# One PSUM bank in place of two for the spread B rows of a Mamba scan, with the small means and variances beside it one state earlier

## What is computed

```python
x = x + conv(_ln_c(x), ...)      # a Mamba block over 4 sequences
t = t + ffn(_ln_t(t), ...)       # top-2 of 8 experts, and a shared expert
def step(h, inputs):             # 256 inner channels, 16 states
    dt_t, B_t, C_t, u_t = inputs
    dA = jnp.exp(dt_t[:, :, None] * A)
    h = dA * h + (dt_t * u_t)[:, :, None] * B_t[:, None, :]
    y = jnp.einsum('bdn,bn->bd', h, C_t)
    return (h, y)
```

## Time and profile before

| | before |
|---|---|
| median of 3 runs | 2801.65 us |
| lowest and highest | 2800.4 and 2802.36 us |
| the profiled execution, its time | 2802.32 us |
| its span, first to last instruction | 2800.7 us |
| around the span | 1.6 us |
| TensorE busy | 2437.4 us, 87% |
| VectorE busy | 1409.5 us, 50% |
| GpSimd busy | 1127.7 us, 40% |
| ScalarE busy | 1012.9 us, 36% |
| mean granted clock of TensorE | 0.962 of 2.4 GHz |

### The profile page before, as it was taken

One profiled execution on the slowest core, in us unless ns is written; L12 is line 12 of the kernel. 1 busy time (PEld: TensorE's weight loads), 2 busy tenths in 40 slices (PEclk: granted clock), 3 DMA queues, 4 the chain that ended last, 5 costly groups with the idle time before them and its releaser, 6 DMA issues.

```text
span 2800.7 us, 28349 instructions
## 1 busy us (share of the span) xinstructions
PE 2437.4 (87%) x7648; PEld 1257.2 (45%) x7649; DVE 1409.5 (50%) x1767; ACT 1012.9 (36%) x1971; POOL 1127.7 (40%) x959
## 2 busy tenths in 40 slices
PE   5788888878888888877999999999999999999962
PEld 3345445444444444444444444444444444444431
DVE  1899999998999999996321111111111111111125
ACT  3776766776667767762100100010011001100000
POOL 2788787787787887874003400000000000000015
PEclk7999999999999999999999999999999999999985
DMA  9212112212122222222024311230202202030026
GB/s 297 71 66 68 64 62 68 66 66 70 60 66 69 66 63 71 66 68 72 28 103 131 117 34 39 97 112 22 112 22 112 112 23 112 26 116 23 22 71 211
DMA packets 92975, 220.27 MB, mean 79 GB/s; under 512 B 11217, under 2 KB 34361, under 8 KB 89537
## 3 DMA queue, kind: packets, MB, share of 16 engines
q1 hardware_dynamic: 77840, 138.79, 15.2%
q0 software_dynamic: 15024, 80.23, 8.1%
HBM read 172.25 MB, written 46.73 MB: 78 GB/s over the span
## 4 chain that ended last, share of the span: by engine, by line
PE 56%; DVE 25%; issue 10%; ACT 5%; POOL 2%; DVEq 1%; DMA 0%; ACTq 0%; SPq 0%; POOLq 0%
PE pair L1442 31%; DVE WALL L1005 15%; PE single L1454 15%; DVE pair L988 8%; PE pair L1323 4%; PE single L1229 2%; PE pair L1224 2%; ACT z L818 1%; POOL WALL L614 1%; PE pair L1424 1%; ACT WALL L770 1%; DVEq L270 1%; PE single L1291 1%; PE pair L1316 0%; DVE X L948 0%
## 5 line engine op out<-in xcount | busy, mean ns | idle before, releaser
L1442 PE MATMUL pair<-WALL,z 128*128 (+1 forms) x1952 | 855.0, 596 | 31.0 <-ACT z L818 29.6
L527 POOL TENSOR_TENSOR WALL<-WALL 128x768 f32<-128x768 f32 x384 | 696.5, 1816 | 243.5 <-DVE WALL L1005 229.2
L1005 DVE TENSOR_TENSOR_SCAN WALL<-WALL,carry,pair 128x384 f32<-128x384 f32 x640 | 613.4, 1000 | 20.5 <-ACT WALL L770 4.2
L1323 PE MATMUL pair<-WALL,ident 128*128 128x384 f32 x1536 | 581.1, 504 | 3.1 <-DVE pair L988 3.1
L1442 PEld LDWEIGHTS pair<-WALL,z 128*128 128x128 f32 x1952 | 366.4, 190 | 483.4 <-issue 480.1
L1127 DVE TENSOR_TENSOR dtu<-dt,pair 128x512 f32<-128x512 f32 x122 | 83.9, 688 | 803.2 <-ACT dt L824 797.1
L770 ACT ACTIVATE WALL<-dt,An 128x384 f32<-128x384 f32 x768 | 424.1, 605 | 75.0 <-DVE WALL L1005 56.5
L988 DVE TENSOR_TENSOR pair<-dtu,pair 128x768 f32<-128x768 f32 x384 | 368.8, 960 | 51.8 <-POOL dtu L456 15.8
L824 ACT ACTIVATE dt<-pair 128x512 f32<-128x512 f32 x122 | 72.8, 597 | 828.4 <-PE pair L1442 828.4
L1323 PEld LDWEIGHTS pair<-WALL,ident 128*128 128x128 f32 x1536 | 293.9, 198 | 138.2 <-issue 22.1
L594 POOL DMA_DIRECT2D WALL<-in_L_ffn_w_dram x21 | 13.9, 666 | 826.3 <-PE single L1454 824.7
(11 more groups left out here) (213 smaller groups left out, 2037.9 us busy)
## 6 DMA issues: line engine op xcount, KB each, us to landing
WALL<-crows SPq DMA_DIRECT2D x192, 384.0 KB, 3.4
WALL<-in_L_ffn_w_dram POOLq DMA_DIRECT2D x24, 2048.0 KB, 13.5
u<-xrows SPq DMA_DIRECT2D x61, 256.0 KB
xrows<-zrow SPq DMA_DIRECT2D x43, 256.0 KB, 2.7
yrows<-expx SPq DMA_DIRECT2D x31, 256.0 KB
yrows<-onex SPq DMA_DIRECT2D x30, 256.0 KB
WALL<-in_L_ffn_sw_dram POOLq DMA_DIRECT2D x3, 2048.0 KB, 13.0
X<-in_x_dram SPq DMA_DIRECT2D x4, 1152.0 KB, 7.8
```

Source lines behind the costliest of these rows:

```text
L527: pool.tensor_tensor(hC[m], hs[:, (NS * j + n) % HRING, :, :], Cs[G % 3][:, n % CG, :].unsqueeze(1).to_broadcast([P, HALF, T]), ALU.mult). ...
L1005: scan = nv.tensor_tensor_scan(hs[:, m, h, :], dA[(NS * j + n) % AHEAD][:, h, :], Dt[:, h, 0:T], init, ALU.mult, ALU.add)
L1323: last = mm(Yt[:, h, 0:T], ident[:, :], hC[n % RING][:, h, :], start=(n == 0), stop=(n == NS - 1))
L1442: last = mm(bank[2 * w + q][:, :], xT[k][:, r, :], WALL[:, ds(off + (w * RR * I + r * I + q * 512), 512)], start=(r == 0), stop=(r == RR - 1))
```

## The change

`Bb` becomes one bank. TensorE, once the product of state n is done, spreads the row of state n + 1 in place of n + 2. VectorE takes the variances in states 1 and 3 (before: 2 and 4), and the two `centre` steps in states 9 and 13 (before: 10 and 14). TensorE still makes the means in states 0, 2, 8 and 12, and all its other work stays in its state.

```diff
--- before.py
+++ after.py
@@ -143,7 +143,7 @@
         single = [ctx.enter_context(nc.psum_tensor(f"single{k}", [P, 512], fp32)) for k in range(2)]
         bank = [pair[k // 2][:, k % 2, :] for k in range(6)] + [single[k][:, :] for k in range(2)]
         Yt, Dt = pair[0], pair[2]
-        Bb = [bank[2], bank[3]]
+        Bb = bank[2]
         M0, M1 = bank[6], bank[7]
         STAT = T
 
@@ -971,22 +971,22 @@
                     for n in range(NS):
                         i = NS * g + n
                         m = (NS * j + n) % HRING
-                        stat = Bb[n % 2][:, STAT:STAT + CP]
+                        stat = Bb[:, STAT:STAT + CP]
                         v.wait_ge(m_B, i + 1)
-                        if front1 and n == 2:
+                        if front1 and n == 1:
                             front_variance(g + 2, stat)
-                        if late and n == 4:
+                        if late and n == 3:
                             back_variance(g - 2, stat)
-                        if front0 and n == 10:
+                        if front0 and n == 9:
                             centre(g + 3, b if j < JC - 3 else b + 1, (j + 3) % JC, f_mean, f_cen, cen, stat, f_seq, g + 3)
-                        if behind and n == 14:
+                        if behind and n == 13:
                             centre(g - 1, bb, bj, b_mean, b_cen, cen2, stat, b_lps, g - 1)
 
                         if n == 0:
                             v.wait_ge(f_dtu, g + 1)
                         after(v, m_h, i)
                         nv.tensor_tensor(Dt[:, :, 0:T], dtu[k][:, :, :],
-                                         Bb[n % 2][:, 0:T].unsqueeze(1).to_broadcast([P, HALF, T]),
+                                         Bb[:, 0:T].unsqueeze(1).to_broadcast([P, HALF, T]),
                                          ALU.mult).then_inc(m_dBu, 1)
 
                         if behind and n == 3:
@@ -1313,7 +1313,7 @@
             pe.wait_ge(s_x, 16 * (B - 1))
 
             def spread(g, j, n):
-                mm(Bb[n % 2][:, 0:T], sel[:, n, :], S[j % 2][:, :], start=True, stop=True).then_inc(m_B, 1)
+                mm(Bb[:, 0:T], sel[:, n, :], S[j % 2][:, :], start=True, stop=True).then_inc(m_B, 1)
 
             def add_y(g, n):
                 pe.wait_ge(m_hC, NS * g + n + 1)
@@ -1328,8 +1328,7 @@
                     last = mm(Yt[:, h, 0:T], Dg[:, h, :], u[k][:, h, :], start=False, stop=False)
                 last.then_inc(m_du, 1)
             pe.wait_ge(f_lo, 1)
-            for n in range(2):
-                spread(0, 0, n)
+            spread(0, 0, 0)
 
             def batch(b, first, last):
                 for j in range(JC):
@@ -1359,12 +1358,11 @@
                             pe.wait_ge(b_x, g)
                             pe.wait_ge(f_cen, g + 4 if front0 else NCH)
                             mean_of(xchunk(bb, bj), b_mean, stat)
-                        if n < NS - 2:
-                            spread(g, j, n + 2)
+                        if n < NS - 1:
+                            spread(g, j, n + 1)
                         elif front:
-                            if n == NS - 2:
-                                pe.wait_ge(f_lo, g + 2)
-                            spread(g + 1, j + 1, n + 2 - NS)
+                            pe.wait_ge(f_lo, g + 2)
+                            spread(g + 1, j + 1, 0)
 
                         if n < 3:
                             if behind:
```

## The result

| | before | changed |
|---|---|---|
| median of 4 runs | 2801.34 us | 2857.19 us |
| lowest and highest | 2800.4 and 2802.36 us | 2852.41 and 2859.09 us |
| the profiled execution, its time and span | 2802.32, 2800.7 us | 2855.74, 2854.1 us |

The ratio is 1.0197, with a 95% interval of 1.0179 to 1.0214. The change makes the kernel 2% slower. The forecast was 2855 us and slower.

What follows compares the result with a forecast made beforehand. VectorE, 95% busy in the scan stage, was taken to set the pace. A 57.75 us wait at the back `centre`, less 4.6 us returned, made 53.2 us on 2802.3: 2855 us, range 2836 to 2872 us.

Steps and rivals of the forecast that it cites:

- Part 1: Scan stage, one bank: the later spread stays hidden behind VectorE's two scans, with 0.5 us to spare; cost nothing.
- rival C: Scan stage: the spread comes late, in all 384 states (near 3055 us) or in part (2873 us); chance 0.06.
- Part 2: Variances in states 1 and 3, front `centre` in state 9: the wait for the spread row covers their means; cost nothing.
- Part 3: Back `centre` in state 13 waits for `gate_logits` in 22 chunks, 1.5 us or, at TensorE's low clock, 3.15; 57.75 us.
- Part 4: From state 13 TensorE has no arrears, so VectorE's old waits at `gate_y` and `centre` vanish; 4.6 us come back.
- The sum: Whole kernel: 57.75 us lost less 4.6 us returned, 53.2 us, giving 2855 us, 1.9% slower.
- B: State 12: only 0 to 8 chunks run at TensorE's low clock; 2830 to 2843 us; chance 0.10.
- A: State 12: nearly every chunk, 18 to 22, runs at TensorE's low clock; 2866 to 2871 us; chance 0.14.
- D: Scan stage: the old waits at `gate_y` and `centre` vanish and nothing replaces them; faster, 2797 us; chance 0.02.
- E: State 13: the back `centre` finds its count reached, so nothing moves; 2802 us; chance 0.02.
- The 22 waits at L924: VectorE's `centre` waits for `gate_logits` behind the scans of state 12, 1.5 or 3 us each, 45 to 65 us total.
- L988 was to wait under 1 us for spreads: Scan stage: VectorE's waits at source line L988 for TensorE's spread row stay under 1 us in total.

## Why the prediction was right

- **Part 1, the bank, at nothing.** Right by itself: one bank alone is at 1.0003. The 0.5 us of cover in a state with a mean held at full clock: from 430 to 690 us of that run, most of it at full clock, VectorE waited 0.2 us in all for a spread. The price given for half clock, 0.75 us, should be 2.87 - 2.15 = 0.72, which makes rival C's 18 us 17.3. The rule on rotating banks in the Trainium skill (Perfetto Trace Analysis, Matmuls) would have had each state pay. The run with one bank alone decides against it here: two scans, 1.92 us, lie between two readings of the bank.
- **Part 2, the variances and the front `centre`, at nothing.** Right within 0.1%: 2805.46 against 2804.35 us.
- **Part 3, the wait of the back `centre`.** The mechanism, its count of 22 and both prices were right: 1.50 us forecast and 1.41 to 1.55 measured, 3.15 forecast and 2.96 to 3.23 measured. The count of slow chunks was wrong: I raised the trace's 13 to 15 for the new idle time behind `gate_logits`, and the profiled execution had 6, the next one 8. The idle time ahead of the mean of state 12 was 1.78 to 2.01 us in all 22 chunks of both kernels, so its length doesn't tell which are slow. The term of 57.75 us measured 42.1.
- **Part 4, what comes back.** This step failed in sign. I took it that VectorE's wait in state 13 would leave TensorE without arrears and gave back 4.6 us. TensorE does start state 13 without arrears, but the low level then falls into states 14 and 15, in nine chunks where before it never reached state 15 for more than 0.3 us. There TensorE has almost a full state of work, and VectorE met the arrears as late spreads, 13.7 us. 3.0 us came back at `gate_y`.
- **The sum.** 57.75 - 4.6 = 53.2 forecast, and 41.2 + 13.2 - 3.0 = 51.4 found, with 53.4 between the spans. The two misses, 16 us at the wait one way and 14 us in part 4 the other, cancel. Both come from where the low level fell: less often into state 12 (6 chunks for 13) and more often behind it, though three chunks had both. The runs don't show that the one must pay for the other, so that the total came so near is luck.
- **The rivals.** B's condition is what happened: 0 to 8 slow chunks, which I gave a chance of 0.10, and both profiled executions, with 6 and 8, are in it. Its price of 2830 to 2843 us did not come, as it too took back 4.6 us and put nothing for late spreads. C had the symptom, the late spread, but not its cause: it wanted the chain of a mean and a spread to outlast the two scans at half clock, while the late spread shown for chunk 15 has no mean ahead of it, took 0.33 us at full clock and came late through TensorE's arrears. A, D and E did not happen.
- **The signs.** The 22 waits at L924 came, but with 42.1 us, just under the 45 to 65 forecast. The new idle time of TensorE is 1.62 us, where the prediction's own numbers give 0.13 + 0.45 + 0.96 = 1.54 and it wrote 1.4. Two signs failed: L988 was to wait under 1 us for spreads and waited 5.4, with the variances 13.7; and "if the scan stage grows by more than the waits at L924 account for" was named as a sign of being wrong, and it grew by 53.4 us for 41.2 at L924. By that sign the account was incomplete, though the time was right.

## What to carry to other kernels

When a read is moved one step earlier, look at every wait that moves with it, above all at those that guard the buffer it writes; here the mean and the spread had cover, and the guard of `cen2` had none. A wait's price is read from the two timelines: the end of what it waits for, plus the hand-over seen elsewhere in the same trace, less the time at which the engine would have come. If the freed resource lets the work that the guard waits for go earlier, as the freed bank did for `gate_logits`, the loss can go with it.

## What the runs showed of the hardware

Which chunks met the 1.2 GHz level was not a property of the program alone: two executions of the changed kernel had 6 and 8 slow chunks in state 12. With one idle place of TensorE filled (state 13) there were 14 and the time was 2863.32 us; with three filled there were none in state 12, 7 left in states 13 and 14, and the time was 2835.18 us. The idle time ahead of state 12 was at most 2.01 us, and TensorE still fell to 0.50 of its clock in 6 of the 22 chunks of the changed kernel and in 13 of 22 before. With VectorE's stall in state 13 and nothing put into TensorE's idle time, the low level reached state 15 (25.6, 17.3 and 23.6 us over all chunks in three profiled executions); without the stall it did not (0.3 us before, 0.0, 0.9 and 0.0 us with one bank and `centre` in state 14, one bank alone, and `gate_logits` in state 11). The Trainium skill (TensorE: Matmul & The Clock Gate, Part 1) says that activity releases the throttle. The run with all three places filled agrees, at 0.99 against 0.96.
